# First expert layer in two passes over token halves, with one half's router in attention's last steps and its state space layer in the second pass

## The reference

```python
h = _layernorm(x) * (1 + ca) + sa;  x = x + ga * _L0_attn_ref(h, ...)   # 16 query heads, 4 key heads, causal
h = _layernorm(x) * (1 + cb) + sb;  x = x + gb * _L0_ffn_ref(h, ...)    # 64 experts of width 32, top 6
# layer 1, with its own sa, ca, ga, sb, cb, gb from L1_c @ L1_wmod
h = _layernorm(x) * (1 + ca) + sa;  x = x + ga * _L1_attn_ref(h, ...)   # state space: h_t = A * h_(t-1) + B x_t
h = _layernorm(x) * (1 + cb) + sb;  x = x + gb * _L1_ffn_ref(h, ...)    # 8 experts of width 512, top 2
```

```python
scores = sigmoid(x_flat @ w_gate);  _, topk_idx = top_k(scores, 6)
w = take(scores, topk_idx);  w = w / w.sum(-1)
pos = cumsum(one_hot(flat_e))[...] - 1;  valid = pos < 128      # an expert's later tokens are dropped
y = silu(x @ w_shared_up gate half) * (value half) @ w_shared_down  +  sum over chosen valid experts, weighted by w
```

## Time and profile before

| | |
|---|---|
| time, 3 runs | 913.78, 921.45 (median), 924.27 us |
| the profiled execution | 921.18 us, its span 919.4 us |
| PE busy | 790.6 us, 4582 matmuls |
| DVE busy | 565.3 us, 1317 instructions |
| ACT busy | 418.9 us |
| POOL busy | 192.8 us |
| DMA | 48.37 MB, mean 53 GB/s |

### The profile page before, as it was taken

One profiled execution on the slowest core, in us unless ns is written; L12 is line 12 of the kernel. 1 busy time (PEld: TensorE's weight loads), 2 busy tenths in 40 slices (PEclk: granted clock), 3 DMA queues, 4 the chain that ended last, 5 costly groups with the idle time before them and its releaser, 6 DMA issues.

```text
span 919.4 us, 13272 instructions
## 1 busy us (share of the span) xinstructions
PE 790.6 (86%) x4582; PEld 646.2 (70%) x4582; DVE 565.3 (61%) x1317; ACT 418.9 (46%) x929; POOL 192.8 (21%) x145
## 2 busy tenths in 40 slices
PE   3787999989999899998998687999995347999992
PEld 3666788877888778887897566888884144666661
DVE  5647758677586775867766584656668962333333
ACT  3456757657577574775754312333332012333320
POOL 1005201142010430102301111332320103333310
PEclk9979999999999999999999688999997657999997
DMA  5000000100001000000000713333305311111104
GB/s 183 1 6 30 2 1 1 35 24 1 1 1 35 24 2 1 1 1 24 2 1 1 289 52 125 122 101 113 113 35 228 137 47 46 38 43 43 46 11 137
DMA packets 16752, 48.37 MB, mean 53 GB/s; under 512 B 2445, under 2 KB 7950, under 8 KB 15536
## 3 DMA queue, kind: packets, MB, share of 16 engines
q1 hardware_dynamic: 13440, 41.37, 12.9%
q0 software_dynamic: 2208, 5.12, 1.9%
q10 hardware_dynamic: 1040, 1.05, 0.4%
HBM read 43.07 MB, written 5.37 MB: 53 GB/s over the span
## 4 chain that ended last, share of the span: by engine, by line
PE 76%; DVE 14%; DMA 3%; ACT 3%; issue 2%; POOL 0%; SPq 0%; DVEq 0%; POOLq 0%; ACTq 0%
PE ps L1203 16%; PE ps L1204 16%; PE ps L1205 15%; PE ps L1527 9%; PE ps L1301 5%; PE ps L1545 4%; DVE mx L855 2%; DVE pT_lo L869 1%; PE ps L1367 1%; DVE stat L770 1%; PE ps L1213 1%; PE ps L1379 1%; PE ps L1537 1%; PE ps L1354 1%; DMA wbc<-combine 1%
## 5 line engine op out<-in xcount | busy, mean ns | idle before, releaser
L585 ACT ACTIVATE prob<-ps,negb,rqs 128x128 f32<-128x128 f32 (+7 forms) x128 | 106.7, 833 | 67.5 <-DVE negb L860 66.6
L574 ACT ACTIVATE pT_hi<-ps 128x512 fp32r<-128x512 f32 (+1 forms) x192 | 88.8, 491 | 64.5 <-PE ps L1301 58.2
L855 DVE TENSOR_REDUCE mx<-ps 128x1 f32<-128x128 f32 (+7 forms) x128 | 96.4, 753 | 26.1 <-PE ps L1293 24.6
L869 DVE TENSOR_TENSOR pT_lo<-ps,pT_hi 128x512 fp32r<-128x512 f32 (+1 forms) x192 | 99.8, 547 | 1.9 <-ACT pT_hi L574 1.8
L444 POOL TENSOR_TENSOR oT_lo<-o_f,oT_hi 128x512 fp32r<-128x512 f32 x32 | 41.3, 1290 | 281.8 <-ACT oT_hi L647 281.8
L1527 PE MATMUL ps<-wgu,xgT 128*128 x184 | 88.6, 605 | 1.0 <-ACT xgT L717 1.0
L1301 PE MATMUL ps<-ident,prob 128*128 128x128 f32 x576 | 86.1, 276 | 0.7 <-DVE qT_lo L889 0.4
L1203 PE MATMUL ps<-pT_hi,v_hi 128*128 128x512 f32 x192 | 72.9, 380 | 13.4 <-DVE pT_lo L869 13.4
L1203 PE MATMUL ps<-kT_hi,qT_hi 128*128 128x512 f32 (+1 forms) x192 | 70.0, 364 | 5.4 <-ACT prob L585 3.6
L1204 PE MATMUL ps<-kT_lo,qT_hi 128*128 128x512 f32 (+1 forms) x192 | 66.7, 347 | 0.0
L1205 PE MATMUL ps<-kT_hi,qT_lo 128*128 128x512 f32 (+1 forms) x192 | 66.5, 346 | 0.0
(11 more groups left out here) (255 smaller groups left out, 1971.0 us busy)
## 6 DMA issues: line engine op xcount, KB each, us to landing
wbc<-combine SPq DMA_DIRECT2D x16, 512.0 KB
wgu<-in_gate_up SPq DMA_DIRECT2D x8, 1024.0 KB, 12.3
w_raw<-in_ffn SPq DMA_DIRECT2D x17, 384.0 KB, 8.9
wdn<-in_down SPq DMA_DIRECT2D x1, 4096.0 KB, 17.4
wqkv_raw<-in_w_attn SPq DMA_DIRECT2D x4, 768.0 KB, 4.2
wo_raw<-in_w_out SPq DMA_DIRECT2D x4, 512.0 KB, 3.3
x<-in_x ACTq DMA_DIRECT2D x1, 1024.0 KB, 7.0
wmod<-in_wmod SPq DMA_DIRECT2D x1, 1024.0 KB, 9.8
```

The costliest lines, as they stand in the source:

```text
L574: nc.scalar.activation(pT_hi[:, unit % NUNITS, 0:nb, qi * P:(qi + 1) * P], ps[:, ROTATING[place % 3], 0:nb * P].rearrange("p (j t) -> p j ...
L585: nc.scalar.activation(prob[:, n % 3, 0:w], ps[:, pair:pair + 2, :].rearrange("p b k -> p (b k)")[:, 0:w], ACT.Exp, bias=negb[:, n % 2:n % ...
L855: nc.vector.reduce_max(mx[:, i:i + 1], ps[:, pair:pair + 2, :].rearrange("p b k -> p (b k)")[:, 0:w], AX.X).then_inc(row_max, 1)
L869: nc.vector.tensor_tensor(pT_lo[dst], ps[:, ROTATING[place % 3], 0:nb * P].rearrange("p (j t) -> p j t", j=nb), pT_hi[dst], ALU.subtract). ...
```

## The change

The expert layer's 34 units keep their work but change their order: units 0 to 16 are the 17 tiles for tokens 0 to 511 (half 0), units 17 to 33 the same tiles for tokens 512 to 1023 (half 1). Around this:

- Weights are loaded, scaled and split for every unit, so 34 times. There are seven buffers (`NW`) and a weight buffer comes free with the unit's `down` (before: with the split). The spread loads are 32 of 256 KB in four buffers (`NC0`).
- Half 0's prelude stands in attention's last steps: statistics at steps 121 to 124, `normalise_rows` on ACT at 125 and 126 (before on DVE), transposes and modulation at 127 and 128, router at 130, ranks and flags at 131 and 132, counts and weights at 133, the whole `up` of unit 0 ahead of step 134, weight transposes at 136. ACT copies the transposed weights out and issues the store (L637).
- Half 1's prelude is spread over units 0 to 13, layer 1's modulation stands at unit 14. Half 0's sums are read at unit 19, and half 0's state space layer stands in units 20 to 33. What is left of half 0 after the last unit is its second normalise, transposes and router.
- The sums use two banks for each half (`SUMS`), so two banks are free for the work above.
- The 4 MB load of `wdn` is cut in eight, issued at every third unit from 6 to 27; the modulation weights come in one load of 1.5 MB.
- Rows that are normalised for the expert gather go to `xn_h`, four tiles wide, used in turn by half 0 and half 1.

The core of the diff (the functions of DVE and ACT that are only cut into halves are left out):

```diff
 (SP)
-            sp.wait_ge(down_done, 2 * (1 + IT0))
+            for u in range(4, UNITS):
+                if u + 3 >= NW and u + 3 < UNITS:
+                    load_weights(u + 3)
+                if u % (1 + IT0):
+                    load_combine(u)
+                if 6 <= u < 6 + 3 * E1 and u % 3 == 0:
+                    e = (u - 6) // 3
+                    sp.dma_start(wdn[:, e, :, :], down1_d[:, e, :, :]).then_inc(w1_loaded, 16)
+            sp.wait_ge(down_done, UNITS)
             for e in range(E1):
                 sp.dma_start(wgu[:, e, :], gate_up_d[:, e, :]).then_inc(w1_loaded, 16)
 
             rows1 = rows1_d.rearrange("(t p) d -> p t d", p=P)
-            for hf in range(2):
-                sp.wait_ge(ln_normed, 3 * NT + 4 * hf + 4)
-                sp.dma_start(rows1[:, 4 * hf:4 * hf + 4, :], xn_b[:, 4 * hf:4 * hf + 4, :]).then_inc(rows_stored, 16)
+            for h in range(2):
+                sp.wait_ge(rows_normed, 16 + 4 * h)
+                if h == 1:
+                    sp.wait_ge(ln_normed, NT + 4)
+                sp.dma_start(rows1[:, 4 * h:4 * h + 4, :], xn_h[:]).then_inc(rows_stored, 16)
 (DVE, units)
+            for u in range(UNITS):
+                gate(u)
+                if u == 0:
+                    dve.wait_ge(y_added, 4 * NG)
+                    link(stats(xt, tiles_of(1)))
+                    variances(tiles_of(1))
+                if u == 1:
+                    root_steps(tiles_of(1), 3)
+                    shifts(tiles_of(1))
...
+                if u == 19:
+                    layer_out_stats(0)
...
+                if u == 25:
+                    dve.wait_ge(gates1_ready, 2)
+                    scan(0)
+                if u == 26:
+                    state_rows(0)
+                if u == 27:
+                    state_stats(0)
...
+                if u == 30:
+                    state_weighted(0)
+                if u == 31:
+                    state_added(0)
+                if u == 32:
+                    link(stats(xt, tiles_of(0)))
+                    variances(tiles_of(0))
+                if u == 33:
+                    root_steps(tiles_of(0), 3)
+                    shifts(tiles_of(0))
+                gated_low(u)
+            layer_out_stats(1)
+            variances(tiles_of(1))
+            root_steps(tiles_of(1), 3)
+            shifts(tiles_of(1))
+            dve.wait_ge(x_kept, 3)
+            dve.wait_ge(rows_stored, 16)
+            dve.wait_ge(ln_transposed, 12)
+            normalise(xt, xn_h, (4, 5))
+            scan(1)
 (ACT, after the units)
+            normalise_rows(3, tiles_of(0))
+            keep_rows(1)
...
+            act.wait_ge(x_kept, 4)
+            act.wait_ge(rows_stored, 16)
+            normalise_rows(4, (6, 7))
 (PE, units)
+            for u in range(UNITS + 2):
+                if u == 0:
+                    mark_banks(0)
+                elif u < UNITS:
+                    if u == 1:
+                        pe.wait_ge(y_added, 4 * NG)
+                        pe.wait_ge(wT_ready, 1)
+                    if u == 1 + IT0:
+                        pe.wait_ge(h_lo, 8)
+                    up(u)
+                if u == 3:
+                    pe.wait_ge(rows_normed, 8)
+                    pe.wait_ge(o_normed, HEADS)
+                    both_rows(1)
...
+                if u == 24:
+                    state_in(0)
+                if u == 26:
+                    state_out(0)
+                if u == 27:
+                    transpose_state(0)
+                if u >= 2:
+                    down(u - 2)
```

More of the change, by code:

```diff
@@ L137, in bank_plan @@
             take("r", m)
+        if n in TRANSPOSE_ROWS:
+            take("rows", TRANSPOSE_ROWS.index(n))
+        if n == ROUTE:
+            take("route", 0)
+        if n == COUNT:
+            take("count", 0)
+        if n == SPREAD:
+            take("spread", 0)
         for half in range(2):
@@ L194, in program @@
         mv = keep("mv", [P, NT, 2])
-        idle = keep("idle", [P, 1])
+        shift = keep("shift", [P, NT])
         rs_in = keep("rs_in", [P, NT * 5])
@@ new lines, in state_added @@
+            def state_added(h):
+                dve.wait_ge(x_shifted, h + 1)
+                for t in tiles_of(h):
+                    ins = nc.vector.scalar_tensor_tensor(x[:, t, :], xn_h[:, t % 4, :], rs_y[:, t:t + 1], x_b[:, t, :],
+                                                         ALU.mult, ALU.add)
+                link(ins)
+            rows = ps[:, SUMS[1] + 1, :].rearrange("p (r d) -> p r d", r=2)
+            sign, size = [zT[:, i, :].rearrange("p (r d) -> p r d", r=2) for i in range(2)]
@@ new lines, in count_chosen @@
+            def count_chosen(h, bank):
+                pe.wait_ge(sel_ready, h + 1)
+                for t in tiles_of(h):
+                    for q in range(t + 1):
+                        ins = nc.tensor.matmul(ps[:, bank, (t % 4) * E0:(t % 4 + 1) * E0],
+                                               (before_b if q == t else ones_b)[:], sel_b[:, q, :], start=(q == 0),
+                                               stop=(q == t), skip_group_check=True)
+                ins.then_inc(counted, 1)
@@ L1469, in _ @@
-            ffn(0, combine0)
-            transpose_input(2)
-            pe.wait_ge(ssm_loaded, 80)
-            pe.wait_ge(x_kept, 1)
-            for hf in range(2):
-                pe.wait_ge(h_full, 10 + 2 * hf)
+                    elif kind == "rows":
+                        bank_free(place)
+                        pe.wait_ge(rows_normed, 4)
+                        transpose_rows(index, bank)
+                    elif kind == "route":
+                        bank_free(place)
+                        pe.wait_ge(gate_loaded, 16)
+                        pe.wait_ge(h_full, 6)
+                        router(wgate, E0, bank, 0)
+                    elif kind == "count":
+                        bank_free(place)
+                        count_chosen(0, bank)
+                    elif kind == "spread":
+                        bank_free(place)
+                        transpose_combine(0, bank)
@@ new lines, in _ @@
+            pe.wait_ge(rows_normed, 16)
+            both_rows(0)
+            pe.wait_ge(h_full, 12)
+            router(wgate1, E1, 0, 0)
+            pe.wait_ge(rows_normed, 18)
+            pe.wait_ge(ln_normed, NT + 2)
+            pe.wait_ge(x_kept, 4)
+            both_rows(1)
+            state_in(1)
+            state_out(1)
+            transpose_state(1)
+            pe.wait_ge(rows_normed, 20)
+            pe.wait_ge(ln_normed, NT + 4)
+            both_rows(1)
+            pe.wait_ge(h_full, 16)
@@ L1500, in _ @@
+            router(wgate1, E1, 0, HT * E1)
             pe.wait_ge(chosen_ready, 1)
```

993 lines of the change are left out of this document (561 added, 432 removed).

## The result

The changed kernel took 933.36 us (median of 4 runs, 931.59 to 933.74), the kernel before 920.51 us beside it. The ratio is 1.0144, with a 95% interval of 1.0083 to 1.0205. The forecast was 913.5 us in a range of 900 to 930: the time lies above the range and on the other side of no change.

A forecast was written before the change was run, and what follows sets the result against it. The prediction took PE as the bound in attention and the steady expert layer, with mostly DVE's work in the tail. From 921.2 it took 15.8 gained up to the last unit and added 8.1 lost in the tail: 913.5 us, range 900 to 930.

The follow-up runs named there:

- e14: Changed kernel with early spread and weight loads reordered, POOL splitting unit 3 before scaling 4 and 5, modulation weights halved behind units 7 and 10: 925.21 us.
- e2: Changed kernel with DVE writing `fb` into the PSUM bank it just read instead of SBUF, so `fc` has one PSUM input: 925.53 us, ratio 1.0079.
- e3: Changed kernel with POOL filling the weights' low part with zeros from unit 7 on instead of computing it: 926.05 us, ratio 1.0094.
- e1: Changed kernel with SP issuing the store of half 0's rows ahead of the eight `wgu` loads: 914.66 us, ratio .9965.
- e8: Changed kernel with `FIRST_UP = 133`, so `up(0)` stands ahead of the counts on PE: 931.16 us, ratio 1.0162.

## What to carry to other kernels

Before a change that doubles an engine's work is called hidden, look not only at whether that engine has time for it, but at which instructions of its neighbour then fall beside it: a margin that is read in rows where the two never met is no margin. And add up the neighbour's side work for every stretch, not only for the one that looks fullest. When a wait is put on a DMA that exists only to free a buffer, look at what stands ahead of it in its queue, and issue it first. A gain that is made ahead of a chain counts only when the loads of the next ten units are still on time; follow them that far before moving a load of a megabyte.

## What the runs showed of the hardware

- A DVE operation on 128 x 512 with both inputs in SBUF took .69 us alone. Beside POOL instructions that read SBUF `fc` took up to 1.73 in the changed kernel and up to 2.35 in e14, `hid_lo` up to 2.81. With one input in PSUM it was .69 in all 32 instances of e2, and beside a zero fill .69 in the two instances of e3.
- Two hardware queues shared the DMA engines packet for packet: 443 packets of 1 KB beside 455 of up to 8 KB in 9 us, and 15.4 us from issue to landing for 512 KB that take 3.1 on empty engines.
- PE's clock fell in some executions and not in others after like waits at the counts: from 570 to 580 us it was 1.00 in the changed kernel (wait 2.20) and in e1 (2.86), .83 in e8 (2.49) and e3 (2.71). A stretch of 10 us at .83 instead of 1.00 costs about 1.7 us, an estimate, and one to three of them in a run of units are a good part of what single runs differ by. What decides it stays open.
